# Two kv buffers, squares on ScalarE, and both layer norms' statistics moved from VectorE to ScalarE in a gated-convolution and mixture-of-experts kernel

## What is computed

```python
x = x + tanh(g_xattn) * conv_attention(ctx, ctx, layernorm(x), ssm_kernel, D)   # first stage
x = x + tanh(g_ffn) * moe(layernorm(x))                                         # second stage

def conv_attention(k, v, q, ssm_kernel, D):      # heads of 8 rows, 512 positions
    kv = einsum('bhil,bhjl->bijhl', k, v)        # products of all pairs of rows; k and v are both ctx
    y = causal_convolution(kv, ssm_kernel) + kv * D
    return einsum('bijhl,bhil->bjhl', y, q)

def layernorm(x):                                # over the 512 positions of a row
    return (x - mean(x)) / sqrt(var(x) + 1e-5)
```

## Time and profile before

| | |
|---|---|
| median of the runs | 770.11 us (770.05 to 771.84) |
| the profiled execution's own time | 769.46 us |
| its span in the profile | 767.5 us |
| TensorE busy | 725.1 us, 94% of the span |
| VectorE, ScalarE, GpSimd busy | 577.8, 431.1 and 381.5 us |

### The profile page before, as it was taken

How to read it: one execution, slowest core, us unless ns; L and a number is a source line. 1 busy time by engine, 2 the same in 40 slices (tenths; PEclk the granted TensorE clock), 3 DMA queues, 4 the chain that set the end, 5 groups by cost and what they waited for, 6 DMA issues and landing times.

```text
span 767.5 us, 15537 instructions
## 1 busy us (share of the span) xinstructions
PE 725.1 (94%) x4602; PEld 675.8 (88%) x4602; DVE 577.8 (75%) x1152; ACT 431.1 (56%) x579; POOL 381.5 (50%) x191
## 2 busy tenths in 40 slices
PE   2899999999999999999999999999999999999993
PEld 2889899989888999999998999889899989999992
DVE  5889898999975469433799588679758985895892
ACT  3444444444432322123789577668758875895882
POOL 2898989888800137021335443344343435544242
PEclk9999999999999999999999999999999999999998
DMA  6658677776522211263466577677646575434200
GB/s 194 224 188 246 226 238 236 229 246 218 207 96 70 56 28 42 42 242 74 129 173 178 116 256 182 176 188 197 176 112 179 139 210 149 94 73 72 42 16 0
DMA packets 47425, 114.32 MB, mean 149 GB/s; under 512 B 7392, under 2 KB 7392, under 8 KB 47360
## 3 DMA queue, kind: packets, MB, share of 16 engines
q1 hardware_dynamic: 34528, 88.62, 34.8%
q0 software_dynamic: 12832, 24.93, 17.3%
HBM read 157.25 MB, written 29.26 MB: 243 GB/s over the span
## 4 chain that ended last, share of the span: by engine, by line
PE 58%; DVE 16%; DMA 8%; issue 7%; ACT 5%; SPq 2%; ACTq 1%; DVEq 1%; POOL 0%; POOLq 0%
PE pair L1196 15%; PE bank L1196 12%; PE pair L1221 10%; PE bank L1221 5%; PE pair L1132 5%; DMA out<-ys,slot_info 4%; DMA raw<-in_weights 3%; PE bank L1090 3%; PE bank L1143 3%; PE pair L1204 2%; DVE st L693 2%; DVE prod L746 2%; DVE bank L751 2%; DVE rows L758 2%; ACT xn L550 2%
## 5 line engine op out<-in xcount | busy, mean ns | idle before, releaser
L1063 DVE TENSOR_TENSOR w_lo<-raw,w_hi 128x1408 fp32r<-128x1408 f32 x94 | 148.8, 1622 | 44.8 <-ACT w_hi L650 44.8
L1319 POOL DMA_INDIRECT tn<-t_rows,slot_info x47 | 71.2, 1516 | 134.1 <-DVE tT_lo L803 117.6
L1330 POOL DMA_INDIRECT out<-ys,slot_info x47 | 86.3, 1836 | 100.3 <-DMA out<-ys,slot_info 70.6
L650 ACT ACTIVATE w_hi<-raw 128x1408 fp32r x94 | 124.9, 1375 | 5.9 <-DMA raw<-in_weights 3.8
L1132 PE MATMUL pair<-kv_hi,toep_hi 128*128 128x288 f32 x320 | 100.5, 314 | 4.4 <-issue 1.9
L1068 DVE TENSOR_TENSOR w_lo<-raw,w_hi 128x1536 fp32r<-128x1536 f32 x47 | 82.4, 1754 | 17.4 <-ACT w_hi L657 17.2
L1132 PE MATMUL pair<-kv_hi,toep_lo 128*128 128x288 f32 x320 | 95.3, 298 | 0.0
L1132 PE MATMUL pair<-kv_lo,toep_hi 128*128 128x288 f32 x320 | 95.1, 297 | 0.0
L1275 POOL TENSOR_TENSOR kv_lo<-kv,kv_hi 128x2304 fp32r<-128x2304 f32 (+1 forms) x16 | 79.6, 4972 | 18.8 <-ACT kv_hi L582 18.8
L657 ACT ACTIVATE w_hi<-raw 128x1536 fp32r x47 | 69.4, 1477 | 15.5 <-DMA raw<-in_weights 15.4
L1330 POOL DMA_INDIRECT out<-ys,own_row x16 | 27.4, 1713 | 82.5 <-ACT ys L638 76.1
(11 more groups left out here) (213 smaller groups left out, 2012.6 us busy)
## 6 DMA issues: line engine op xcount, KB each, us to landing
raw<-in_weights SPq DMA_DIRECT2D x94, 704.0 KB
raw<-in_weights SPq DMA_DIRECT2D x47, 768.0 KB
toep_hi<-kpad_hi SPq DMA_DIRECT2D x16, 512.0 KB, 4.1
toep_lo<-kpad_lo SPq DMA_DIRECT2D x16, 512.0 KB, 6.0
cx<-in_ctx SPq DMA_DIRECT2D x16, 384.0 KB, 6.3
stage<-in_weights SPq DMA_DIRECT2D x16, 272.0 KB, 4.5
xt<-in_x SPq DMA_DIRECT2D x16, 256.0 KB, 6.4
xr<-in_x SPq DMA_DIRECT2D x16, 256.0 KB, 6.5
```

What stands on the lines that cost most here:

```text
L650: act.activation(w_hi[s % 2][:, a:b], raw[:, bass.ds(half + a, b - a)], ACT.Copy).then_inc(hi_ok[n_], 1)
L1063: dve.tensor_tensor(w_lo[s % 2][:, a:b], raw[:, bass.ds(half + a, b - a)], w_hi[s % 2][:, a:b].bitcast(F32), ALU.subtract).then_inc(lo_ok[ ...
L1319: pool.indirect_dma_start(out=tn[o % 2][:], out_offset=None, in_=t_rows, in_offset=bass.IndirectOffsetOnAxis(ap=slot_info[:, 3 * i:3 * i + ...
L1330: pool.indirect_dma_start(out=out, out_offset=bass.IndirectOffsetOnAxis(ap=rows, axis=0), in_=ys[o % 2][:], in_offset=None, bounds_check=R ...
```

## The change

A second `kv` buffer lets `form` run one tile further ahead. `form` on GpSimd (and VectorE for tile 0) leaves out the squares, and a new function `square` on ScalarE writes them. The context loads go one tile further ahead. The statistics of both layer norms leave VectorE: ScalarE takes a pass over the 512 elements with `Copy`, scaled by -1/512 and with an accumulated output (minus the mean), waits for itself, takes a pass with `Square`, the bias being that output (512 times the variance), waits for itself, and takes the root with a scale of 1/512. Orders on VectorE, ScalarE and GpSimd are changed. The diff, cut where lines repeat:

```diff
-        kv = sb("kv", [P, BLOCKS * GROUPS * PAIRS], F32, one)
+        kv = sb2("kv", [P, BLOCKS * GROUPS * PAIRS], F32, one)
+        spent = sb("spent", [P, L], F32, one)
...
         def form(eng, t):
-            wait(eng, kvl2_ok, t)
+            wait(eng, kvl2_ok, t - 1)
...
-            eng.tensor_tensor(view(kv[:], 0, [[PAIRS * BATCH, g], [hb, 4], [1, hb]]),
+            eng.tensor_tensor(view(kv[p][:], hb, [[PAIRS * BATCH, g], [hb, 3], [1, hb]]),
...
@@ SyncE
             load(At(0), "toep")
             load(At(1), "ctx")
             load(At(1), "x")
+            sp.wait_ge(kv_ok, 2)
+            sp.wait_ge(square_ok, 1)
+            load(At(2), "ctx")
             load(At(1), "toep")
...
             def turn(t):
+                if not t.within(TILES - 3, TILES):
+                    wait(sp, kv_ok, (t + 2) * 2)
+                    wait(sp, square_ok, t + 2)
+                    load(t + 3, "ctx")
                 if ahead:
-                    wait(sp, kv_ok, (t + 1) * 2)
-                    load(t + 2, "ctx")
                     wait(sp, xn_ok, t + 1)
                     load(t + 2, "x")
@@ ScalarE
+            def stats(src, mv, ok, t):
+                p = t.odd
+                act.activation(spent[:], src[p][:], ACT.Copy, scale=-1.0 / L, accum_out=mv[p][:, 0:1]).then_inc(ok, 1)
+                wait(act, ok, t * 2 + 1)
+                act.activation(spent[:], src[p][:], ACT.Square, bias=mv[p][:, 0:1],
+                               accum_out=mv[p][:, 1:2]).then_inc(ok, 1)
             def std_x(t):
+                wait(act, x_in[t.odd], (t.half() + 1) * 16)
+                wait(act, rstd1, (t - 1) * 2)
+                stats(xt, mv1, stat1, t)
                 wait(act, stat1, (t + 1) * 2)
                 act.activation(sd1[..][:, 0:1], mv1[..][:, 1:2], ACT.Sqrt, bias=small[:, 0:1], scale=1.0 / L)
...
+            def square(t):
+                wait(act, kvl2_ok, t - 1)
+                wait(act, ctx_in[p], (t.half() + 1) * 16)
+                act.activation(view(kv[p][:], 0, [[PAIRS * BATCH, g], [1, hb]]),
+                               view(cx[p][:], 0, [[EXT * BATCH, g], [1, hb]]), ACT.Square).then_inc(square_ok, 1)
...
+            square(At(0))
             act.wait_ge(kpad_ok, 1)
             act.activation(krow_hi[:], krow[:], ACT.Copy).then_inc(krowh_ok, 1)
             split_kv_hi(At(0))
             std_x(At(0))
             norm_x(At(0))
             q_copy(At(0))
+            square(At(1))
             def turn(t):
+                split_shared(t)
+                if not last:
+                    split_kv_hi(t + 1)
+                    std_x(t + 1)
+                if not first:
+                    std_x2(t - 1)
+                if not t.within(TILES - 2, TILES):
+                    square(t + 2)
+                if not first:
+                    norm_x2(t - 1)
+                if not last:
+                    norm_x(t + 1)
+                    q_copy(t + 1)
+                if not first:
+                    tT_copy(t - 1)
@@ VectorE
             form(dve, At(0))
-            stats_x(At(0))
...
                 products(t, 0)
                 if not first:
                     residual(t - 1)
                 if not first and not t.within(1, 2):
                     logits_copy(t - 2)
+                if not last:
+                    scale_x(t + 1)
                 products(t, 1)
                 if not first:
                     scale_x2(t - 1)
-                if not last:
-                    stats_x(t + 1)
                 products(t, 2)
-                if not last:
-                    scale_x(t + 1)
                 products(t, 3)
@@ GpSimd
             split_kv(At(0))
+            form(pool, At(1))
             def turn(t):
-                if not t.within(TILES - 1, TILES):
-                    form(pool, t + 1)
                 split_shared(t)
                 if not t.within(TILES - 1, TILES):
                     split_kv(t + 1)
+                if not t.within(TILES - 2, TILES):
+                    form(pool, t + 2)
```

More of the change, by code:

```diff
@@ L204, in program @@
         x2 = sb2("x2", [P, L], F32, one)
-        st1, st2 = sb2("st1_", [P, 6], F32, one), sb2("st2_", [P, 6], F32, one)
         mv1, mv2 = sb2("mv1_", [P, 3], F32, one), sb2("mv2_", [P, 3], F32, one)
         sd1, sd2 = sb2("sd1_", [P, 2], F32, one), sb2("sd2_", [P, 2], F32, one)
-        kv = sb("kv", [P, BLOCKS * GROUPS * PAIRS], F32, one)
+        kv = sb2("kv", [P, BLOCKS * GROUPS * PAIRS], F32, one)
         kv_hi = sb2("kv_hi", [P, BLOCKS * GROUPS * PAIRS], F32R, one)
@@ L273, in program @@
         stat1, std1, rstd1, xn_ok = sem("stat1"), sem("std1"), sem("rstd1"), sem("xn_ok")
-        q_turned, q_ok, kv_ok = sem("q_turned"), sem("q_ok"), sem("kv_ok")
+        q_turned, q_ok, kv_ok, square_ok = sem("q_turned"), sem("q_ok"), sem("kv_ok"), sem("square_ok")
         kvh_ok, kvl_ok, kvl2_ok = sem("kvh_ok"), sem("kvl_ok"), sem("kvl2_ok")
@@ L304, in pairs @@
                 turn(At(t))
-            n = (TILES - 4) // 2
+            n = (TILES - 6) // 2
             with eng.Fori(0, n) as i:
@@ L308, in pairs @@
                     turn(At(o, 2, i, n))
-            turn(At(TILES - 1))
+            for t in range(TILES - 3, TILES):
+                turn(At(t))
         FREE_H = 8
@@ L364, in form @@
             p = t.odd
-            wait(eng, kvl2_ok, t)
-            if t.within(1, 2):
+            wait(eng, kvl2_ok, t - 1)
+            if t.within(2, 3):
                 eng.wait_ge(kvl_ok, 1)
@@ L369, in form @@
             g, hb = BLOCKS * 2, HD * BATCH
-            eng.tensor_tensor(view(kv[:], 0, [[PAIRS * BATCH, g], [hb, 4], [1, hb]]),
-                              view(cx[p][:], 0, [[EXT * BATCH, g], [0, 4], [1, hb]]),
-                              view(cx[p][:], 0, [[EXT * BATCH, g], [BATCH, 4], [1, hb]]),
+            eng.tensor_tensor(view(kv[p][:], hb, [[PAIRS * BATCH, g], [hb, 3], [1, hb]]),
+                              view(cx[p][:], 0, [[EXT * BATCH, g], [0, 3], [1, hb]]),
+                              view(cx[p][:], BATCH, [[EXT * BATCH, g], [BATCH, 3], [1, hb]]),
                               ALU.mult).then_inc(kv_ok, 1)
-            eng.tensor_tensor(view(kv[:], 4 * hb, [[PAIRS * BATCH, g], [1, hb // 2]]),
+            eng.tensor_tensor(view(kv[p][:], 4 * hb, [[PAIRS * BATCH, g], [1, hb // 2]]),
                               view(cx[p][:], 0, [[EXT * BATCH, g], [1, hb // 2]]),
@@ L536, in _ @@
             act.activation(small[:, 3:4], small[:, 0:1], ACT.Sqrt)
+            def stats(src, mv, ok, t):
[4 more added lines that the diff above has]
+                               accum_out=mv[p][:, 1:2]).then_inc(ok, 1)
             def std_x(t):
+                wait(act, x_in[t.odd], (t.half() + 1) * 16)
+                wait(act, rstd1, (t - 1) * 2)
+                stats(xt, mv1, stat1, t)
                 wait(act, stat1, (t + 1) * 2)
-                act.activation(sd1[t.odd][:, 0:1], mv1[t.odd][:, 1:2], ACT.Sqrt, bias=small[:, 0:1]).then_inc(std1, 1)
+                act.activation(sd1[t.odd][:, 0:1], mv1[t.odd][:, 1:2], ACT.Sqrt, bias=small[:, 0:1],
+                               scale=1.0 / L).then_inc(std1, 1)
             def std_x2(t):
+                wait(act, x2_ok, t + 1)
+                wait(act, rstd2, (t - 1) * 2)
+                stats(x2, mv2, stat2, t)
                 wait(act, stat2, (t + 1) * 2)
-                act.activation(sd2[t.odd][:, 0:1], mv2[t.odd][:, 1:2], ACT.Sqrt, bias=small[:, 0:1]).then_inc(std2, 1)
+                act.activation(sd2[t.odd][:, 0:1], mv2[t.odd][:, 1:2], ACT.Sqrt, bias=small[:, 0:1],
+                               scale=1.0 / L).then_inc(std2, 1)
             def norm_x(t):
@@ L581, in split_kv_hi @@
                 wait(act, kv_ok, (t + 1) * 2)
-                act.activation(kv_hi[p][:], kv[:], ACT.Copy).then_inc(kvh_ok, 1)
+                wait(act, square_ok, t + 1)
+                act.activation(kv_hi[p][:], kv[p][:], ACT.Copy).then_inc(kvh_ok, 1)
+            def square(t):
+                p = t.odd
+                wait(act, kvl2_ok, t - 1)
+                if t.within(2, 3):
+                    act.wait_ge(kvl_ok, 1)
+                wait(act, ctx_in[p], (t.half() + 1) * 16)
+                g, hb = BLOCKS * 2, HD * BATCH
+                act.activation(view(kv[p][:], 0, [[PAIRS * BATCH, g], [1, hb]]),
+                               view(cx[p][:], 0, [[EXT * BATCH, g], [1, hb]]), ACT.Square).then_inc(square_ok, 1)
             def split_shared(t):
@@ L595, in _ @@
             q_copy(At(0))
+            square(At(1))
             def turn(t):
-                if not t.within(0, 1):
+                first, last = t.within(0, 1), t.within(TILES - 1, TILES)
+                split_shared(t)
[3 more added lines that the diff above has]
+                if not first:
                     std_x2(t - 1)
-                split_shared(t)
-                if not t.within(TILES - 1, TILES):
-                    split_kv_hi(t + 1)
```

(26 more changed lines are left out.)

## The result

The changed kernel takes **780.38 us** (median of 6 runs, 777.92 to 781.61); the kernel before, run beside it, 769.6 (6 runs, 766.29 to 771.84). The ratio is **1.0141, interval 1.0117 to 1.0165**: slower by 1.4%, 11 us. The forecast was 783.4 with a range of 773 to 791, so sign and mechanism held and the size was 3 us too large. The profiled execution took 780.56, its span 778.8 against 767.5.

A forecast was written before the change was run, and what follows sets the result against it. The kv, kv_hi, kv_lo loop was taken to bound the tile at 13.0 us; the change was to replace it by a 13.4 us loop. 5.6 + 2.2 + 5.4 + 0.7 = +13.9 on 769.46 gives 783.4 us, range 773 to 791.

The forecast's parts named there:

- The forecast mechanism: First-stage tiles: VectorE's scale_x(t+1) waits for ScalarE's root ahead of products(t,1), 13.4 us a tile against 12.97; chance 0.82.
- S: Time from the start of a layer norm's passes on ScalarE to the root: 2.0 us, between 1.67 and 2.3.
- A': Start of turn_q(t+1) on TensorE, forecast 11.39 us plus S after A: 13.4 us a tile.
- A: Start of turn_q(t) on TensorE, from which the tile's loop over ScalarE, VectorE and TensorE was counted.
- The other legs: Loop parts besides S: 4.52 us to ScalarE's passes, 2.67 over VectorE, 4.20 over TensorE to turn_q(t+1).
- 14 x 13.3 - 0.5: Time from conv(1,0) to conv(15,0), forecast with 13.4 a tile: 187.0 us against 181.5 before, +5.4.
- First tiles and clock: conv(1,0) later behind stage 0, +5.6 us; TensorE at half clock after waiting in tile 0, +2.2 (bounds 0 to 2.2).
- the faster rival: scale_x finds the root done, so TensorE's 12.0 us sets the tile: 758 us; needs S about 0.6; chance 0.10.
- tile 0 was to start 1.7 late: S replaces the root in tile 0, putting kv_lo(0) back by 1.7 us, hidden while TensorE stands waiting.
- The end: After tile 15 the second norm's statistics and root, 1.00 and 0.29 us, give way to S: +0.7.
- The second stage: Work after the first stage: untouched, only starting later by the whole.
- The table rival: Square outside the root's table on ScalarE: two loads a norm, S 4.6 us, time 825 us; chance 0.04.

The follow-up runs named there:

- experiment 1: The changed kernel with VectorE's scale_x(t+1) put behind products(t,1) instead of ahead of it: 762.13 us, ratio 0.9918 to the kernel before.
- the pair of 3: The changed kernel with one extra unread 512-element Copy pass on ScalarE: ahead of std_x's statistics 788.56 us, ahead of norm_x 777.16 us.
- experiment 2: The changed kernel with scale_x(t+1) moved behind products(t,1) in turn 0 alone: 778.07 us, ratio 1.0128 to the kernel before.
- the changed kernel's second profile: The changed kernel itself, unaltered, run again beside the kernel with only its kv part: 778.39 us, ratio 1.0128 to the kernel before.
- the best order of experiment 5: Changed kernel with scale_x behind products(t,1), split_kv_hi, std_x, split_kv ahead of split_shared in turn 0, gate(t-2) behind sum_rows(t-1,3): 754.9 us, ratio 0.9847.
- the first order of experiment 5: Changed kernel with scale_x behind products(t,1) and, every turn, split_kv_hi and std_x (ScalarE), split_kv (GpSimd) ahead of split_shared: 768.68 us, ratio 0.9982.

## Why the prediction came out, step by step

- **The forecast mechanism was right**: the root's place ahead of products(t,1). The one moved line of experiment 1, and the pair of 3, show it. The marks named for it are there, some a little smaller: VectorE's wait is 1.7 (2 forecast), TensorE's idle time before sum_rows(t,1) 0.8 (over 1), no wait for kv_lo, no table load, stage 0 at 23.3.
- **The term that was mis-sized: S, in the tiles.** I took 2.0 between 1.67 and 2.3; it is 1.90. The accumulator read is an instruction of 0.2 us, 0.22 to 0.24 start to start, a little above my 0.17, while passes and hand-overs came in below my sizes. A' = A + 11.39 + 1.90 gives 13.29, and the tile is 13.30. The other legs were right one by one (89.03 is turn_q in the tile shown above): 4.49 us to the passes (4.52 forecast), 2.69 over VectorE (2.67) and 4.22 over TensorE (4.20), so the match isn't errors that cancel. With it the prediction's 14 x 13.3 - 0.5 is 185.7, and 185.69 was measured: +4.2 instead of +5.4.
- **First tiles and clock** were +5.6 and +2.2, together 7.8, and are 7.6. That they meet within 0.2 is in part luck: stage 0 was there 1.6 later (1.5 forecast) in this profile, but 0.7 later in the changed kernel's second one, where conv(1,0) starts at 36.29. The clock was the guess with the widest bounds, 0 to 2.2. After 6.3 us without work five transposes took 1.33 instead of 0.77 (as in the chain of experiment 2) and 24 matmuls 4.70 instead of 3.19: 2.1 us more, most of it at the lower level.
- **Missed, and hidden here:** form(2) and kv_hi(2) behind kv_lo(1), the second late start of experiment 2. In the changed kernel turn 0 is slow enough to cover it, so the sum wasn't hurt; the faster rival's 758 would have been too low for it.
- **Missed, no cost:** tile 0 was to start 1.7 late. The root was 1.4 late, but kv_lo on VectorE was faster (below), so conv began about 0.3 late. Nothing depended on it. GpSimd's larger `form` instruction fell from 4.32 to 3.53 us, 0.8 and not 1.1, which GpSimd's idle time covered.
- **The end** was forecast at +0.7 and is +0.5: from the passes to the root it is 1.91 in place of 1.29, +0.6, and x2 of tile 15 came 0.15 earlier after conv(15,0). **The second stage**, the -0.9 above, was taken as unchanged. The same stretch takes 521.6 in the changed kernel's second profile against 523.7 in the first, so 0.9 is less than it differs by between two profiles of one kernel.
- **The faster rival** came near in its price, but its condition didn't hold: with the wait off the path, experiment 1 is at 762 and the best order of experiment 5 at 755, where it said 758. It needed S near 0.6 in the order of the change, and S was 1.90. The table rival fell: Copy, Square, Identity and the root alternate on ScalarE, and no table load stands between 6 and 222 us.

## What to carry to other kernels

Before moving work from a busy engine to one with idle time, write down the loop that the result closes: from the first instruction that waits for it, through every instruction queued behind, back to where the moved work begins. Idle time on the receiving engine says nothing if the consumer stands early in its own queue; moving the consumer behind the work that another engine needs was worth 2% here, for one moved line. A second buffer breaks a loop only as long as no queue order chains its users again, as the first order of experiment 5 did.

## What the runs showed that was not expected

**kv_lo on VectorE** in tile 0 has two inputs from SBUF and 1280 elements. Before, then after, with GpSimd's own part of the same step (timelines):

```profile
12.21 2.35 POOL L1275 TENSOR_TENSOR kv_lo<-kv,kv_hi 128x1024 fp32r<-128x1024 f32 x1 [10.48 <-ACT kv_hi L582]
13.35 2.56 DVE L763 TENSOR_TENSOR kv_lo<-kv,kv_hi 128x1280 fp32r<-128x1280 f32 x1
```

```profile
12.07 2.34 POOL L1297 TENSOR_TENSOR kv_lo<-kv,kv_hi 128x1024 fp32r<-128x1024 f32 x1 [10.35 <-ACT kv_hi L605]
14.81 1.43 DVE L788 TENSOR_TENSOR kv_lo<-kv,kv_hi 128x1280 fp32r<-128x1280 f32 x1
```

It takes 1.43 us with GpSimd idle and 2.56 when it starts 1.2 us before GpSimd's instruction ends: 1.13 more, nearly all of the overlap, with GpSimd's time unchanged. The Trainium skill (SBUF — State Buffer, Who interferes with whom) has a VectorE instruction with two SBUF inputs contend with a GpSimd instruction that reads SBUF; by that rule, the trace agrees.

**An accumulator output on ScalarE** shows in the trace as an instruction of its own, 0.19 to 0.21 us. Mean, variance and root of 512 elements take 1.90 us there, and with the statistics on VectorE it was 1.29 from their start to the end of the root.
